# Splitting the residual addition of the last layer between ScalarE and GpSimd

## The chip, the cores and the metric

The kernel runs on one core of a Trainium2 chip. The metric is the device time of one execution in microseconds (us). Before the change it is 1846.93 us, the median of three runs (1844.24, 1846.93 and 1849.25).

## What is computed

Four layers follow one another on x, two batches of 2048 tokens of 512 values: cross attention, a routed block, a second cross attention, and a ternary feed-forward. Each is added to x behind a gate. The change is in the last one:

```python
def act_quant(x):
    scale = 127.0 / jnp.clip(jnp.max(jnp.abs(x), axis=-1, keepdims=True), 1e-05)
    return jnp.clip(jnp.round(x * scale), -128, 127) / scale
...
h = bit_linear(x, w1)                     # int8-like tokens, ternary weights, 512 -> 2048
h = depthwise_conv1d(h.transpose(0, 2, 1), conv_w, conv_b)   # three taps along the tokens
h = jax.nn.silu(h.transpose(0, 2, 1))
return bit_linear(h, w2)                  # 2048 -> 512
...
x = x + jnp.tanh(g_ffn[1]) * _L1_ffn_ref(_layernorm(x, axis=-1), ...)
```

The output product of a token has to be multiplied by that token's unit (its largest magnitude over 127, times the gate and the mean of the weights), and then added to the residual x.

## The kernel before

`ternary_layer` takes the 4096 tokens as eight tiles of 512, and a tile's 2048 hidden channels as eight pairs of 128, one pair to a **slot**. Slot p of tile n is written (n, p) here. All engines run the same double loop over n and p, each with its own instructions, and meet at semaphores. Nothing reorders them: each engine does its queue as it is written.

In a slot the work for different tiles overlaps:

- VectorE: `biggest` (line 2805) takes the maximum of the pair four slots back, from the PSUM tensor YT. `scale` (2787) moves this slot's hidden pair from PSUM to `hs`. `right_taps` (2796, two instructions, "the taps" below) adds the third tap to the pair of two slots back, reading `hs` and Y in SBUF. In slots 4 to 7, `quantise` (2823) turns one quarter of the previous tile into int8. In slots 6, 0, 2 and 4 (`ADD`), `add_out` (2831) multiplies one quarter of an output, read from its PSUM bank OP, by its unit and adds the residual R. At the end of slot 3 three small instructions (2811 to 2817) make the units.
- GpSimd: the centre tap of the even half (2697, `E_centre`), the edges (2683), and then the addition of both centre taps to Y (2705), 128 x 1024, which waits for ScalarE's taps.
- ScalarE: three taps (2724, 2731, 2734), the copy of turned tokens in slots 0 and 1 (2711), SiLU of the pair two slots back (2745), and in slots 5, 6, 7 and 0 the cast of a quarter from int8 to bf16 (`to_bf16`, 2717).
- TensorE, whose queue is about one slot ahead: `turn_y` (2629) transposes a finished pair into YT, for VectorE's `biggest`. `project_in` (2610) makes a hidden pair. In its slots 7, 1, 3 and 5, `project_out` (2620) makes a quarter of an output with 16 matmuls, in the single bank OP. It waits for the bf16 quarter and for `o_ok`, the addition that frees the bank.

The quarters of a tile's output are called c0 to c3. Those of tile n come in slots (n+1, 6), (n+2, 0), (n+2, 2) and (n+2, 4). SyncE stores a tile when its four additions are counted in `o_ok`, then loads R anew for the tile after the next. Behind the eighth tile the loops run on for two more rounds, the tail, where the last tile (n = 7) is quantised, multiplied and added.

These are the lines on which the order rests:

```python
QUANT, CAST, OUT, ADD = (4, 5, 6, 7), (5, 6, 7, 0), (7, 1, 3, 5), (6, 0, 2, 4)
...
need(pe, o_ok, SUB * n + c)                       # project_out
...
dve.wait_ge(o_mm, SUB * n + c + 1)                # add_out
dve.scalar_tensor_tensor(out=R[n % 2][:, c, :], in0=OP[:, :], scalar=f2[n % 2][:, c:c + 1],
                         in1=R[n % 2][:, c, :], op0=ALU.mult, op1=ALU.add).then_inc(o_ok, 1)
```

Of the kernel before, what the change touches and what calls it, by code (L numbers as in the profile page):

```python
# [7 lines left out]
ALU = mybir.AluOpType  # L8
ACT = mybir.ActivationFunctionType
# [2458 lines left out]
def ternary_layer(nc, io, cst, mean, last):  # L2468

    tg = cst["gates"][:, 3:4]  # L2470
    with stage_semaphores(nc, "E_") as sem, ExitStack() as ctx:
        sb = lambda n, s, d=F32: ctx.enter_context(nc.sbuf_tensor("E_" + n, s, d))
        MP, NBUF, LAG, FOLD = MC // 2, 4, 2, 4
        w1q, w2q = sb("w1q", [P, KD, DH2], BF16), sb("w2q", [P, MC, D], BF16)
        cw, cb = sb("cw", [P, MC, 3]), sb("cb", [P, MC])
# [3 lines left out]
        R = [sb(f"res{i}", [P, SUB, D]) for i in range(2)]  # L2479
        HQ, XH = sb("hq", [2 * STEPS, D], BF16), sb("xh", [P, KD, 2 * STEPS], BF16)  # L2480
        rsq, rsh, hh = sb("rs_q", [2 * STEPS, 1]), sb("rs_halo", [P, 2 * STEPS]), sb("hh", [P, MC, 2 * STEPS])
        hs = [sb(f"hs{i}", [P, 2, TILE + 2]) for i in range(NBUF)]
        U = [sb(f"centre{i}", [P, 2, TILE]) for i in range(2)]
        Y = [sb("y0", [P, MC, TILE])]
# [2 lines left out]
        a2, un, ru = sb("a2", [P, SUB]), sb("unit", [P, SUB]), sb("ru", [P, SUB])  # L2487
        mg = sb("mean_gate", [P, 1])
        f2 = [sb(f"f2_{i}", [P, SUB]) for i in range(2)]

        pb = lambda n, s, d=F32: ctx.enter_context(nc.psum_tensor("E_" + n, s, d))
        HP, YT = pb("HP", [P, 2, 2, TILE]), pb("YT", [P, SUB, 2, P])
        SBK, OP = pb("SB", [P, TILE]), pb("OP", [P, TILE])
# [10 lines left out]
        xq_in, rs_in, r_in, stored = ([sem(f"{n}{i}") for i in range(2)] for n in ("xq_in", "rs_in", "r_in", "stored"))  # L2504
        hq_in, h_tr, xh_ok, hb_mm, hh_ok = sem("hq_in"), sem("h_turned"), sem("xh_ready"), sem("halo_made"), sem("halo_kept")
        x_tr, x_te = sem("x_transposed"), sem("xT_ready")
        h_mm, h_s, h_halo = sem("h_made"), sem("h_scaled"), sem("h_edges")
        tl, ce, co, t0, t2, sil = (sem(n) for n in ("tap_left", "centre_even", "centre_odd", "taps_added", "tap_right", "silu"))
        y_tr, amk, a2_ok, un_ok, ru_ok, f_ok = (sem(n) for n in (
            "y_turned", "amax_pair", "token_max", "unit_ok", "ru_ok", "f_ok"))  # L2510
        sp_mm, q8, qb, o_mm, o_ok = sem("ru_spread"), sem("y_int8"), sem("y_bf16"), sem("out_made"), sem("out_added")

        QUANT, CAST, OUT, ADD = (4, 5, 6, 7), (5, 6, 7, 0), (7, 1, 3, 5), (6, 0, 2, 4)
        r_dr, out_dr = tile_view(io["x3_d"]), tile_view(io["out"])
# [64 lines left out]
        def _(pe):  # L2579
# [34 lines left out]
            def project_out(n, c):  # L2614

                pe.wait_ge(w2_in, 16)
                pe.wait_ge(qb, SUB * n + c + 1)
                need(pe, o_ok, SUB * n + c)
                for k in range(MC):
                    mm = pe.matmul(OP[:, :], yb[:, k, c * P:(c + 1) * P], w2q[:, k, :], start=k == 0, stop=k == MC - 1)  # L2620
                mm.then_inc(o_mm, 1)
# [55 lines left out]
        @block.gpsimd  # L2677
        def _(pool):
            def halo(n, p):

                i, t = MP * n + p, n % 2 * LAPS + n // 2
                need(pool, t2, 2 * (i - NBUF + 1))
                pool.tensor_tensor(hs[i % NBUF][:, :, 0:TILE + 2:TILE + 1], hh[:, 2 * p:2 * p + 2, t:2 * STEPS:STEPS],
                                   cst["ones"][:, 0:4].rearrange("p (a t) -> p a t", a=2), ALU.mult).then_inc(h_halo, 1)

            for c in range(SUB):
                last.scale(pool, c)
            pool.wait_ge(cw_ok, 1)
            pool.wait_ge(conv_in, 32)
            pool.wait_ge(hh_ok, 1)  # L2690
            halo(0, 0)
            for n in range(STEPS):
                for p in range(MP):
                    i = MP * n + p
                    pool.wait_ge(h_s, i + 1)
                    need(pool, t0, i - 1)
                    pool.tensor_scalar(U[i % 2][:, 0, :], hs[i % NBUF][:, 0, 1:TILE + 1], cw[:, 2 * p, 1:2],  # L2697
                                       cb[:, 2 * p:2 * p + 1], ALU.mult, ALU.add).then_inc(ce, 1)
                    if i + 1 < MP * STEPS:
                        halo((i + 1) // MP, (i + 1) % MP)  # L2700
                    pool.wait_ge(tl, 2 * (i + 1))
                    pool.wait_ge(co, i + 1)
                    pool.wait_ge(ce, i + 1)
                    y = Y[n % 2][:, 2 * p:2 * p + 2, :]
                    pool.tensor_tensor(y, y, U[i % 2][:, :, :], ALU.add).then_inc(t0, 1)  # L2705

        @block.scalar
        def _(act):
# [4 lines left out]
            def to_bf16(n, c):  # L2713
                act.wait_ge(q8, SUB * n + c + 1)
                need(act, o_mm, SUB * (n - 1) + c + 1)
                toks = slice(c * P, (c + 1) * P)
                act.activation(yb[:, :, toks], y8[:, :, toks], ACT.Copy).then_inc(qb, 1)  # L2717

            def products(n, p):
# [9 lines left out]
                if i == MP:  # L2729
# [4 lines left out]
                act.activation(Y[n % 2][:, m, :], hs[i % NBUF][:, 1, 0:TILE], ACT.Identity,  # L2734
                               bias=cb[:, m:m + 1], scale=cw[:, m, 0:1]).then_inc(tl, 1)

            def unit_out(n):
                act.wait_ge(un_ok, n + 1)
                need(act, o_ok, SUB * (n - 1))
                act.activation(f2[n % 2][:, :], un[:, :], ACT.Copy, scale=mg[:, :]).then_inc(f_ok, 1)  # L2740

            def silu(i):
# [19 lines left out]
            for n in range(STEPS + 2):  # L2762
                for p in range(MP):
                    i = MP * n + p
                    if n < STEPS:
                        products(n, p)
                    if n + 1 < STEPS and p < 2:
                        keep_xT(n + 1, p)
                    if 0 <= i - LAG < MP * STEPS:
                        silu(i - LAG)  # L2770
                    if p in CAST:
                        if p == CAST[0] and 1 <= n <= STEPS:
                            unit_out(n - 1)
                        s = n - 1 if p else n - 2
                        if 0 <= s < STEPS:
                            to_bf16(s, CAST.index(p))

        @block.vector
        def _(dve):
# [46 lines left out]

            def add_out(n, c):
                dve.wait_ge(o_mm, SUB * n + c + 1)
                dve.wait_ge(r_in[n % 2], 16 * (n // 2 + 1))
                dve.wait_ge(f_ok, n + 1)  # L2830
                dve.scalar_tensor_tensor(out=R[n % 2][:, c, :], in0=OP[:, :], scalar=f2[n % 2][:, c:c + 1],  # L2831
                                         in1=R[n % 2][:, c, :], op0=ALU.mult, op1=ALU.add).then_inc(o_ok, 1)
# [22 lines left out]
            for n in range(STEPS + 2):  # L2855
                for p in range(MP):
                    i = MP * n + p
                    if 0 <= i - FOLD < MP * STEPS:
                        biggest(i - FOLD)
                    if n < STEPS and i > 0:  # L2860
                        scale(n, p)
                    if 0 <= i - LAG < MP * STEPS:
                        right_taps(i - LAG)
                    if 1 <= n <= STEPS:
                        if p == FOLD - 1:
                            units(n - 1)
                        if p in QUANT:
                            quantise(n - 1, QUANT.index(p))
                    if p in ADD:
                        done = n - 1 if p == ADD[0] else n - 2  # L2870
                        if 0 <= done < STEPS:
                            add_out(done, ADD.index(p))


# [38 lines left out]
```

## Time and profile before

| | |
|---|---|
| median of three runs | 1846.93 us |
| the profiled execution's own time | 1849.65 us |
| its span | 1848.0 us |
| busy over the span: TensorE, VectorE, ScalarE, GpSimd | 85%, 69%, 48%, 31% |
| the last layer's tiles | from about 1465 us to the end |
| taps at line 2796 | 128, mean 874 ns |
| additions at line 2831 | 32, mean 745 ns, 23.8 us in all |
| idle time of VectorE just before them | 22.4 us, of which 15.3 us behind 1776 us |

The page gives each engine's busy time over the whole span, and the last layer is only its last fifth. So the shares of the whole say little here, and a round of eight slots in the middle of the layer is read one instruction at a time. In the timeline a row gives the start, how long it took, the engine, the line, the operation, what it writes from what it reads, and, in brackets, how long its engine stood idle before it and what ended that.

### The profile page before, as it was taken

Reading aid. Unit: us, or ns where it says so; the run is one execution under the profiler, and the core shown is the slowest. Engines: PE = TensorE matmul, PEld = TensorE weight load, DVE = VectorE, ACT = ScalarE, POOL = GpSimd, SP = SyncE. Lnnn points to the kernel's source line nnn. Section 1 sums busy time; section 2 is a strip of 40 time slices with the busy share of each in tenths; the row PEclk is TensorE's granted clock in tenths of the full one; section 3 lists DMA queues with packets and bytes.
Section 4 is the critical chain, followed back from the end, with each engine's and each line's share of the span. In section 5 each row is a group of like instructions: output and inputs, shape, how many; then the busy total and the mean of one; then the engine's idle time right before and its main releaser. Section 6 shows DMA issues by size and latency. Waiting matters only on the chain. (4 is left out here: it accounts for less than half of the span.)

```text
span 1848.0 us, 25690 instructions
## 1 busy us (share of the span) xinstructions
PE 1572.4 (85%) x9526; PEld 956.2 (52%) x9559; DVE 1272.5 (69%) x2051; ACT 890.3 (48%) x1438; POOL 580.8 (31%) x558
## 2 busy tenths in 40 slices
PE   4788889888778889747999999999998868888886
PEld 3444444443346657533666665666664534444443
DVE  3367779788542546434577766777666599999995
ACT  3355555455444436325333343333432377777763
POOL 3114332233310002113121120211201297777770
PEclk9899999999878889868999999999999899999999
DMA  4112112212623424340001211012010330222111
GB/s 157 45 47 92 65 50 71 90 69 92 243 85 102 173 95 142 119 166 22 24 24 58 68 36 59 23 58 72 9 58 29 121 120 29 70 76 77 52 46 46
DMA packets 73155, 142.34 MB, mean 77 GB/s; under 512 B 8289, under 2 KB 17653, under 8 KB 72778
## 3 DMA queue, kind: packets, MB, share of 16 engines
q1 hardware_dynamic: 72074, 137.55, 21.6%
q0 software_dynamic: 960, 3.15, 0.5%
q8 instruction: 80, 1.31, 0.3%
q14 instruction: 41, 0.34, 0.1%
HBM read 97.67 MB, written 43.01 MB: 76 GB/s over the span
## 5 line engine op out<-in xcount | busy, mean ns | idle before, releaser
L2705 POOL TENSOR_TENSOR E_y<-E_y,E_centre 128x1024 f32<-128x1024 f32 x64 | 151.2, 2362 | 9.8 <-ACT E_y L2734 7.6
L1322 ACT ACTIVATE D_oT<-D_OB 128x512 fp32r<-128x512 f32 x64 | 38.3, 598 | 226.6 <-DVE D_OB L1663 226.6
L2620 PE MATMUL E_OP<-E_w2q,E_yb 128*128 128x512 bf16 x509 | 124.8, 401 | 25.0 <-issue 18.9
L2697 POOL TENSOR_SCALAR E_centre<-E_hs,E_cw,E_cb 128x512 f32<-128x512 f32 x64 | 108.6, 1696 | 57.5 <-DVE E_hs L2787 57.2
L2610 PE MATMUL E_HP<-E_xT,E_w1q 128*128 128x512 bf16 x482 | 120.1, 388 | 2.5 <-ACT E_xT L2711 0.4
L1628 DVE TENSOR_TENSOR D_q_low<-D_PJ,D_q_high 128x512 fp32r<-128x512 f32 x62 | 42.9, 692 | 114.8 <-ACT D_q_high L1298 114.8
L1400 PE MATMUL D_PJ<-D_xT_high,D_wq_high 128*128 128x512 f32 x248 | 105.5, 425 | 9.2 <-DVE D_wq_low L1635 7.2
L2796 DVE SCALAR_TENSOR_TENSOR E_y<-E_hs,E_cw,E_y 128x512 f32<-128x512 f32 x128 | 106.9, 874 | 0.0
L2620 PEld LDWEIGHTS E_OP<-E_w2q,E_yb 128*128 128x128 bf16 x512 | 51.4, 102 | 91.9 <-issue 42.7
L1400 PE MATMUL D_PJ<-D_xT_high,D_wq_low 128*128 128x512 f32 x248 | 98.8, 399 | 0.0
L1400 PE MATMUL D_PJ<-D_xT_low,D_wq_high 128*128 128x512 f32 x248 | 98.6, 398 | 0.0
L487 PE MATMUL A_TX<-A_wo,A_oT 128*128 128x512 f32 x176 | 90.9, 642 | 7.1 <-PEq L962 7.1
L2629 PE MATMUL E_YT<-ident,E_y 128*128 128x128 f32 x512 | 68.4, 277 | 25.1 <-DVE E_am L2805 21.2
L731 ACT ACTIVATE A_probs<-A_SC 128x512 f32<-128x512 f32 x128 | 65.9, 601 | 46.9 <-PE A_SC L830 46.9
L2724 ACT ACTIVATE E_centre<-E_hs,E_cw 128x512 f32<-128x512 f32 x64 | 46.1, 720 | 84.0 <-DVE E_hs L2787 82.0
L1408 PE MATMUL D_ZB<-D_wo_high,D_oT 128*128 128x512 f32 x240 | 84.0, 411 | 2.2 <-DVE D_rz L1677 2.2
L402 POOL TENSOR_TENSOR A_rstd<-A_var,minus_half 128x1 f32<-128x1 f32 x32 | 29.8, 931 | 172.0 <-DVE A_var L541 172.0
L1408 PE MATMUL D_PJ<-D_wo_high,D_oT 128*128 128x512 f32 x240 | 80.7, 397 | 0.0
L2629 PEld LDWEIGHTS E_YT<-ident,E_y 128*128 128x128 f32 x512 | 58.5, 142 | 41.2 <-issue 20.8
L769 PE MATMUL A_PJ<-A_xT_high,A_wq_high 128*128 128x512 f32 x120 | 58.1, 484 | 25.3 <-POOL A_xT_low L648 18.6
L2787 DVE TENSOR_TENSOR E_hs<-E_HP,E_rs 128x1024 f32<-128x1024 f32 x64 | 77.5, 1211 | 2.9 <-PE E_HP L2610 2.9
L1439 PE MATMUL D_OB<-D_probs,D_V 128*32 128x512 f32 x512 | 71.7, 633 | 9.0 <-DVE D_oT L1669 9.0
(402 smaller groups left out, 4152.5 us busy)
## 6 DMA issues: line engine op xcount, KB each, us to landing
A_x<-in_x SPq DMA_DIRECT2D x8, 1024.0 KB, 5.4
A_res<-in_x SPq DMA_DIRECT2D x8, 1024.0 KB, 5.4
xn_d<-A_xn SPq DMA_DIRECT2D x8, 1024.0 KB, 4.7
x_d<-A_res SPq DMA_DIRECT2D x8, 1024.0 KB, 5.5
W_raw<-in_w1T SPq DMA_DIRECT2D x16, 512.0 KB, 3.6
W_raw<-in_w2T SPq DMA_DIRECT2D x16, 512.0 KB, 3.7
D_x<-x_d SPq DMA_DIRECT2D x8, 1024.0 KB, 5.5
D_res<-x_d SPq DMA_DIRECT2D x8, 1024.0 KB, 6.2
```

Of the source, the lines that this page charges most:

```text
L487: mm = pe.matmul(out_bank(n, c), oT[n % 2][:, k, c * P:(c + 1) * P], wo[:, k, :], start=k == 0, stop=k == QT - 1)
L731: act.activation(pr[:, g, :], SC[:, g, :], ACT.Exp, scale=scale).then_inc(s_ex, 1)
L1400: mm = pe.matmul(bank[:, :], w[:, k, m * P:(m + 1) * P], x[:, k, :], start=k == 0 and x is xh and w is wqh, stop=k == KD - 1 and x is xl)
L1408: mm = pe.matmul(bank, o[i][:, k, c * P:(c + 1) * P], w[half][:, k, :], start=k == 0 and o is oh and w is woh, stop=k == OT - 1 and o is ol)
L1439: mm = pe.matmul(OB[g * PV:(g + 1) * PV, :], V[:, par, v:v + PV], pr[:, g, :], start=True, stop=True)
L2610: mm = pe.matmul(HP[:, i % 2, e, :], w1q[:, k, m * P:(m + 1) * P], XT[n % 2][:, k, :], start=k == 0, stop=k == KD - 1)
L2620: mm = pe.matmul(OP[:, :], yb[:, k, c * P:(c + 1) * P], w2q[:, k, :], start=k == 0, stop=k == MC - 1)
L2629: mm = pe.transpose(YT[:, c, e, :], Y[i // MP % 2][:, 2 * (i % MP) + e, c * P:(c + 1) * P], ident[:, :])
L2697: pool.tensor_scalar(U[i % 2][:, 0, :], hs[i % NBUF][:, 0, 1:TILE + 1], cw[:, 2 * p, 1:2], cb[:, 2 * p:2 * p + 1], ALU.mult, ALU.add).then ...
L2705: pool.tensor_tensor(y, y, U[i % 2][:, :, :], ALU.add).then_inc(t0, 1)
L2787: dve.tensor_tensor(hs[i % NBUF][:, :, 1:TILE + 1], HP[:, i % 2, :, :], RS[n % 2][:, :].rearrange("p (a t) -> p a t", a=1).to_broadcast([P ...
L2796: dve.scalar_tensor_tensor(out=Y[n % 2][:, m, :], in0=hs[i % NBUF][:, e, 2:TILE + 2], scalar=cw[:, m, 2:3], in1=Y[n % 2][:, m, :], op0=ALU ...
```

## The change

For the first seven tiles the addition leaves VectorE. ScalarE's `scale_out` multiplies the bank OP by the unit into one of two new SBUF buffers, `scaled`. GpSimd's `add_scaled` adds that buffer to R. TensorE may refill OP when ScalarE has read it (`o_sc`), and SyncE still waits for `o_ok`, which GpSimd now counts. The last tile keeps VectorE's `add_out`. Both new steps stand at the end of their slot, in the slots of `ADD`.

```diff
+        scaled = [sb(f"out_scaled{i}", [P, D]) for i in range(2)]
...
 def project_out(n, c):
-                need(pe, o_ok, SUB * n + c)
+                if n == STEPS - 1 and c:
+                    pe.wait_ge(o_ok, SUB * n + c)
+                else:
+                    need(pe, o_sc, SUB * n + c)
...
 GpSimd
+            def add_scaled(n, c):
+                r = R[n % 2][:, c, :]
+                pool.wait_ge(o_sc, SUB * n + c + 1)
+                pool.wait_ge(r_in[n % 2], 16 * (n // 2 + 1))
+                pool.tensor_tensor(r, r, scaled[c % 2][:, :], ALU.add).then_inc(o_ok, 1)
...
                         pool.tensor_tensor(y, y, U[i % 2][:, :, :], ALU.add).then_inc(t0, 1)
+                    if p in ADD:
+                        done = n - 1 if p == ADD[0] else n - 2
+                        if 0 <= done < STEPS - 1:
+                            add_scaled(done, ADD.index(p))
...
 ScalarE
+            def scale_out(n, c):
+                act.wait_ge(o_mm, SUB * n + c + 1)
+                act.wait_ge(f_ok, n + 1)
+                need(act, o_ok, SUB * n + c - 1)
+                act.activation(scaled[c % 2][:, :], OP[:, :], ACT.Copy, scale=f2[n % 2][:, c:c + 1]).then_inc(o_sc, 1)
...
                             to_bf16(s, CAST.index(p))
+                    if p in ADD:
+                        done = n - 1 if p == ADD[0] else n - 2
+                        if 0 <= done < STEPS - 1:
+                            scale_out(done, ADD.index(p))
...
 VectorE
 def add_out(n, c):
+                dve.wait_ge(o_ok, SUB * n + c)
...
-                        if 0 <= done < STEPS:
+                        if done == STEPS - 1:
                             add_out(done, ADD.index(p))
```

GpSimd's queue over the slots 0, 1 and 2 of a tile, before (centre tap, edges, addition to Y):

```order
L2697 TENSOR_SCALAR E_centre<-E_hs,E_cw,E_cb 128x512
L2683 TENSOR_TENSOR E_hs<-E_hh,ones 128x2x2
L2705 TENSOR_TENSOR E_y<-E_y,E_centre 128x1024
L2697 TENSOR_SCALAR E_centre<-E_hs,E_cw,E_cb 128x512
L2683 TENSOR_TENSOR E_hs<-E_hh,ones 128x2x2
L2705 TENSOR_TENSOR E_y<-E_y,E_centre 128x1024
```

The same place in the changed kernel, from the addition to Y of slot 0:

```order
L2717 TENSOR_TENSOR E_y<-E_y,E_centre 128x1024
L2701 TENSOR_TENSOR E_res<-E_res,E_out_scaled 128x512
L2709 TENSOR_SCALAR E_centre<-E_hs,E_cw,E_cb 128x512
L2688 TENSOR_TENSOR E_hs<-E_hh,ones 128x2x2
L2717 TENSOR_TENSOR E_y<-E_y,E_centre 128x1024
L2709 TENSOR_SCALAR E_centre<-E_hs,E_cw,E_cb 128x512
L2688 TENSOR_TENSOR E_hs<-E_hh,ones 128x2x2
L2717 TENSOR_TENSOR E_y<-E_y,E_centre 128x1024
L2701 TENSOR_TENSOR E_res<-E_res,E_out_scaled 128x512
```

The new addition stands behind the slot's addition to Y and ahead of the next slot's centre tap, in every second slot here (slots 0, 2, 4 and 6).

ScalarE's queue in slot 0 of a tile and at the start of slot 1, in the changed kernel (2740 to 2750 the three taps, 2727 the turned tokens, 2767 SiLU, 2733 the cast):

```order
L2740 ACTIVATE E_centre<-E_hs,E_cw 128x512
L2747 ACTIVATE E_y<-E_hs,E_cw 128x512
L2750 ACTIVATE E_y<-E_hs,E_cb,E_cw 128x512
L2727 ACTIVATE E_xT<-E_SB 128x1024
L2767 ACTIVATE E_y<-E_y 128x1024
L2733 ACTIVATE E_yb<-E_y 128x16x128
L2757 ACTIVATE E_out_scaled<-E_OP,E_f_0 128x512
L2740 ACTIVATE E_centre<-E_hs,E_cw 128x512
```

The scaling stands behind the cast of quarter c3, and the next slot's taps behind the scaling. Before, the taps followed the cast at once.

## Rows read from the trace of the kernel before

**Rows 1.** Busy time in one round; columns: stretch, length, PE, PEld, DVE, ACT, POOL, PEclk, DMA, GB/s

```profile
1602.57:1647.14 44.57, 38.34 (x210) 21.02 (x212) 42.52 (x44) 32.90 (x40) 33.95 (x25) 0.96 0.18 66
```

**Rows 2.** Timeline of VectorE, (n, 0) to (n, 5), one round

```profile
1633.56 0.75 DVE L2831 SCALAR_TENSOR_TENSOR E_res<-E_OP,E_f,E_res 128x512 f32<-128x512 f32 x1 [0.61 <-PE E_OP L2620]
1634.43 1.23 DVE L2805 TENSOR_REDUCE E_am<-E_YT 128x4 f32<-128x1024 f32 x1
...
1640.30 2.64 DVE L2796 SCALAR_TENSOR_TENSOR E_y<-E_hs,E_cw,E_y 128x512 f32<-128x512 f32 x2
...
1643.54 1.23 DVE L2805 TENSOR_REDUCE E_am<-E_YT 128x4 f32<-128x1024 f32 x1
...
1645.81 1.41 DVE L2796 SCALAR_TENSOR_TENSOR E_y<-E_hs,E_cw,E_y 128x512 f32<-128x512 f32 x2
...
1650.11 1.52 DVE L2796 SCALAR_TENSOR_TENSOR E_y<-E_hs,E_cw,E_y 128x512 f32<-128x512 f32 x2
1651.55 2.27 DVE L2823 TENSOR_TENSOR E_y<-E_y,E_SB 128x2048 int8<-128x2048 f32 x1
1653.75 0.74 DVE L2831 SCALAR_TENSOR_TENSOR E_res<-E_OP,E_f,E_res 128x512 f32<-128x512 f32 x1
1654.41 1.21 DVE L2805 TENSOR_REDUCE E_am<-E_YT 128x4 f32<-128x1024 f32 x1
```

**Rows 3.** Timeline of TensorE in the same round

```profile
1617.27 5.29 PE L2620 MATMUL E_OP<-E_w2q,E_yb 128*128 128x512 bf16 x16 [3.15 <-issue]
...
1633.35 1.04 PE L2629 MATMUL E_YT<-ident,E_y 128*128 128x128 f32 x8
...
1642.46 1.04 PE L2629 MATMUL E_YT<-ident,E_y 128*128 128x128 f32 x8
```

**Rows 4.** Timeline of GpSimd, slots 1 to 4 of the same round

```profile
1636.89 1.70 POOL L2697 TENSOR_SCALAR E_centre<-E_hs,E_cw,E_cb 128x512 f32<-128x512 f32 x1 [0.75 <-DVE E_hs L2787]
...
1639.36 2.37 POOL L2705 TENSOR_TENSOR E_y<-E_y,E_centre 128x1024 f32<-128x1024 f32 x1 [0.60 <-ACT E_y L2734]
...
1643.59 2.36 POOL L2705 TENSOR_TENSOR E_y<-E_y,E_centre 128x1024 f32<-128x1024 f32 x1
...
1648.04 2.37 POOL L2705 TENSOR_TENSOR E_y<-E_y,E_centre 128x1024 f32<-128x1024 f32 x1 [0.18 <-ACT E_y L2734]
```

**Rows 5.** Timeline of GpSimd, the second centre tap of the first tile

```profile
1474.57 0.76 POOL L2697 TENSOR_SCALAR E_centre<-E_hs,E_cw,E_cb 128x512 f32<-128x512 f32 x1
```

**Rows 6.** Timeline of ScalarE, end of slot 0 and slot 1

```profile
1635.45 1.90 ACT L2717 ACTIVATE E_yb<-E_y 128x2048 bf16<-128x2048 int8 x1
1637.25 0.71 ACT L2724 ACTIVATE E_centre<-E_hs,E_cw 128x512 f32<-128x512 f32 x1
...
1638.47 0.81 ACT L2734 ACTIVATE E_y<-E_hs,E_cb,E_cw 128x512 f32<-128x512 f32 x1
```

**Rows 7.** Line 1322, ScalarE reading a PSUM bank; durations min/median/max in ns

```profile
L1322 ACT ACTIVATE D_oT<-D_OB x64: 597/597/601, 844.9 to 1445.5; 128x512 fp32r<-128x512 f32 x64
```

**Rows 8.** Line 1230, an addition on GpSimd; the same columns

```profile
L1230 POOL TENSOR_TENSOR D_res<-D_res,D_bo x32: 1260/1292/1440, 846.7 to 1412.3; 128x512 f32<-128x512 f32 x32
```

**Rows 9.** Timeline of the tail, (8, 0) to (9, 0)

```profile
1810.09 1.89 ACT L2717 ACTIVATE E_yb<-E_y 128x2048 bf16<-128x2048 int8 x1
...
1812.01 5.22 PE L2620 MATMUL E_OP<-E_w2q,E_yb 128*128 128x512 bf16 x16
...
1820.77 3.40 PE L2620 MATMUL E_OP<-E_w2q,E_yb 128*128 128x512 bf16 x15
...
1823.07 1.91 ACT L2717 ACTIVATE E_yb<-E_y 128x2048 bf16<-128x2048 int8 x1 [2.94 <-DVE E_y L2823]
...
1825.11 3.61 PE L2620 MATMUL E_OP<-E_w2q,E_yb 128*128 128x512 bf16 x16 [0.94 <-ACT E_yb L2717]
...
1830.16 3.61 PE L2620 MATMUL E_OP<-E_w2q,E_yb 128*128 128x512 bf16 x16 [1.44 <-DVE E_res L2831]
```

**Rows 10.** TensorE alone in one stretch; columns: stretch, length, PE busy, PEclk, DMA, GB/s

```profile
1617.00:1623.00 6.00, 5.73 (x22) 0.72 0.56 209
```

More of the change, by code:

```diff
@@ L2510, in ternary_layer @@
             "y_turned", "amax_pair", "token_max", "unit_ok", "ru_ok", "f_ok"))
-        sp_mm, q8, qb, o_mm, o_ok = sem("ru_spread"), sem("y_int8"), sem("y_bf16"), sem("out_made"), sem("out_added")
+        sp_mm, q8, qb, o_mm, o_sc, o_ok = (sem(n) for n in (
+            "ru_spread", "y_int8", "y_bf16", "out_made", "out_scaled", "out_added"))
         QUANT, CAST, OUT, ADD = (4, 5, 6, 7), (5, 6, 7, 0), (7, 1, 3, 5), (6, 0, 2, 4)
@@ L2691, in _ @@
             halo(0, 0)
-            for n in range(STEPS):
+            def add_scaled(n, c):
[3 more added lines that the diff above has]
+                pool.tensor_tensor(r, r, scaled[c % 2][:, :], ALU.add).then_inc(o_ok, 1)
+            for n in range(STEPS + 1):
                 for p in range(MP):
                     i = MP * n + p
[L2695 to L2705, printed above, removed]
+                    if n < STEPS:
+                        pool.wait_ge(h_s, i + 1)
+                        need(pool, t0, i - 1)
+                        pool.tensor_scalar(U[i % 2][:, 0, :], hs[i % NBUF][:, 0, 1:TILE + 1], cw[:, 2 * p, 1:2],
+                                           cb[:, 2 * p:2 * p + 1], ALU.mult, ALU.add).then_inc(ce, 1)
+                        if i + 1 < MP * STEPS:
+                            halo((i + 1) // MP, (i + 1) % MP)
+                        pool.wait_ge(tl, 2 * (i + 1))
+                        pool.wait_ge(co, i + 1)
+                        pool.wait_ge(ce, i + 1)
+                        y = Y[n % 2][:, 2 * p:2 * p + 2, :]
+                        pool.tensor_tensor(y, y, U[i % 2][:, :, :], ALU.add).then_inc(t0, 1)
+                    if p in ADD:
+                        done = n - 1 if p == ADD[0] else n - 2
+                        if 0 <= done < STEPS - 1:
+                            add_scaled(done, ADD.index(p))
         @block.scalar
@@ L2735, in products @@
                                bias=cb[:, m:m + 1], scale=cw[:, m, 0:1]).then_inc(tl, 1)
+            def scale_out(n, c):
[3 more added lines that the diff above has]
+                act.activation(scaled[c % 2][:, :], OP[:, :], ACT.Copy, scale=f2[n % 2][:, c:c + 1]).then_inc(o_sc, 1)
             def unit_out(n):
                 act.wait_ge(un_ok, n + 1)
-                need(act, o_ok, SUB * (n - 1))
+                need(act, o_sc, SUB * (n - 1))
                 act.activation(f2[n % 2][:, :], un[:, :], ACT.Copy, scale=mg[:, :]).then_inc(f_ok, 1)
```

## The prediction

> **What bounds the kernel now.** I read the page first (the last layer is the last fifth of the span), then the busy time of one round, then the waits of VectorE in it, then the timelines of the five engines over that round, because a share of busy time does not say which of two nearly full engines a slot waits for.
>
> In a round of eight slots VectorE is busy for 42.5 of 44.6 us, TensorE for 38.3, GpSimd for 34.0 and ScalarE for 32.9 [rows 1]. By these sums an addition taken from VectorE, four of them in a round, should shorten it. The timelines say otherwise, in three ways.
>
> First, **two of the four additions stand in a shadow of TensorE**. The addition of c1 waited 0.61 us for its product and began at 1633.56, and the next `biggest` began at 1634.43, just when TensorE had turned a pair for it: that transpose ran from 1633.35 to 1634.39, behind the product [rows 2, 3]. Without the addition `biggest` begins at the same moment. c0 behaves in the same way one slot after its product, and its product is late because the cast before it is late (3.15 us idle ahead of it) and because it took 5.29 us where others take 3.61 [rows 3, 9]. The granted clock was 0.72 in that stretch [rows 10], against 0.96 over the round [rows 1].
>
> Second, c2 is in a shadow too. `biggest` of slot 3 began at 1643.54, and the transpose for it ended at 1643.50 [rows 2, 3].
>
> Only c3 is in the open: 1653.75 to 1654.41, 0.66 us, with its transpose long done [rows 2].
>
> Third, **GpSimd and the taps exclude each other**. The two taps of a slot take 1.41 us together, but 2.64 us where they began at 1640.30 under GpSimd's addition to Y, which ran from 1639.36 to 1641.73. They ended 1.21 us behind its end, as if they had begun just about there [rows 2, 4]. The addition itself is never longer than its 2.36 us. The other way round, the centre tap takes 1.70 us when it begins with VectorE's taps (1636.89, the usual case), and 0.76 us when it does not [rows 4, 5]. `biggest`, `scale`, `quantise` and `add_out`, which read at most one operand from SBUF (the other is in PSUM), keep their durations under GpSimd's work. In slots 1 to 4 GpSimd has hardly any slack: its addition of slot 2 ends at 1645.95, when the taps of slot 3 (1645.81) begin, and that of slot 3 at 1650.41, when the taps of slot 4 (1650.11) do, which already costs them 0.11 us [rows 2, 4].
>
> **The change, part by part.** The price of each new step: the scaling on ScalarE, between 0.60 us (a read of a PSUM bank without a scale by token, [rows 7]) and 0.71 us (a tap with a scale by partition, [rows 6]). I take 0.65. The addition on GpSimd reads two operands from SBUF: between 1.18 us (half of 2.36, [rows 4]) and 1.44 us, with a median of 1.29 [rows 8]. I take 1.27. Taken away: 28 additions of 0.66 us on VectorE, 18.5 us of engine time, of which by the above only the seven of c3 lie open, and c1 to c3 of the seventh tile lie in the tail.
>
> Now one round, in the times of the trace, from an undisturbed slot 7 on.
>
> - Slot 0, ScalarE. The scaling of c1 stands behind the cast of c3, which ends at 1637.35 [rows 6], though its product was done at about 1633.4. So it runs from 1637.3 to 1637.95. Slot 1's taps follow at 1637.95, 0.7 us late, and end at 1639.98 instead of 1639.28.
> - GpSimd stands idle at the end of slot 0 for the scaling. Its addition of c1 runs from 1638.0 to 1639.3, where slot 1's centre tap began at 1636.89. The centre tap, now outside the taps, takes 0.76 and the edges 0.2, so the addition to Y begins at about 1640.25 instead of 1639.36 and ends at 1642.6.
> - VectorE's taps of slot 2 come at 1640.30, 0.05 us behind it, and are held until 1642.6. They end 1.21 us later, at 1643.8, and `biggest` begins at 1643.75 (instructions of VectorE overlap by 0.08 us, [rows 2]): 0.2 us late.
> - GpSimd, slot 2: centre tap under the held taps 1.70, edges 0.2, addition to Y from 1644.5 to 1646.85. VectorE's taps of slot 3, due at 1646.0, are held until then, and end at 1648.06 instead of 1647.22: 0.85 us late.
> - GpSimd adds c2 from 1648.05 to 1649.3, centre tap and edges to 1650.3, addition to Y to 1652.65. VectorE's taps of slot 4, due 4.30 us behind those of slot 3 [rows 2], now at 1650.97, are held until 1652.65. `quantise` begins at 1653.8 instead of 1651.55: **2.25 us late**. If GpSimd's addition of c2 goes ahead of the held taps of slot 3 instead of behind, the taps of slot 3 lose 1.25 us more and those of slot 4 as much less, with the same sum within 0.2 us.
> - Then c3's addition is missing, 0.66 us. Slot 5 begins **1.6 us later than before**. GpSimd's addition of c3 ends about when slot 5's taps begin, and GpSimd has caught up by slot 6. From slot 5 on the cast of c0, its product and slot 7 follow VectorE's `scale` at fixed distances, so nothing takes the loss back.
>
> What GpSimd's delay and the held taps cost is thus 2.25 us, what is saved 0.66, net 1.55 to 1.6 in a round. The slots 0 to 4 with these additions come in the rounds of tiles n = 2 to 7: 6 x 1.55 = **9.3 us**. The ends of the range: with the cheap prices (0.60 and 1.18) GpSimd is 0.14 us earlier behind c1 and another 0.09 behind c2: 1.3 net, 7.9 us. With the costly ones (0.71 and 1.44) it is 0.23 and 0.17 later, and if VectorE is first by a hair at 1640.30, GpSimd waits there for one tap or both (0.7 to 1.4 us) and passes on what VectorE did not lose, some 0.5: 2.45 net, 14.7 us.
>
> The row on the centre tap can be weighed against a rule. The Trainium skill (SBUF — State Buffer, Who interferes with whom) says that a VectorE instruction with two SBUF inputs and a GpSimd instruction that reads SBUF exclude each other, and that the second to start is blocked fully until the first ends. For the taps the trace agrees (2.64 us). By it a centre tap under both taps would take 1.2 + 0.76 = 1.99 us, where the row has 1.70. The sum here goes by the row; by the rule each round would lose 0.3 us more, 1.8 us in all, and the estimate would be about 1860 us.
>
> **The tail.** The product of c2 of the seventh tile began at 1812.01. Its bank is now free when c1 has been scaled, behind the cast that runs from 1810.09 to 1811.98 [rows 9]: 1812.6. That passes through the last units to the product at 1820.77, 0.7 us later. Then the scaling of c3 (slot 4) stands in ScalarE's queue ahead of the first cast of the last tile (slot 5), and waits for that product: it ends at 1825.1, is read to 1825.8, and the cast that ran from 1823.07 ends at 1827.7. The product that began at 1825.11 begins at about 1827.8, and the next one, at 1830.16 before, waits for its addition and begins at 1832.3 [rows 9]. That is **2.1 us**; behind it the chain is as before. SyncE's store and the load of R move with `o_ok` by two or three us, and R is used a tile later.
>
> **The sum.** 9.3 + 2.1 = 11.4 us on the profiled execution, 1849.65 to about 1861. The median of the runs is 2.7 us lower; I add to that: 1846.93 + 11.4 = **1858.3 us**. With the ends of the terms this case alone spans 1855 to 1864.
>
> **The rivals.** A measurement of this kernel tells about 0.3%, 5.5 us, from no change.
>
> 1. *The clock steps in further.* TensorE stands idle longer in each round, and the product that begins after an idle stretch took 1.68 us more at the lower clock [rows 3, 9]. If a second product in each of six rounds, one on the chain (c1 or c2), does so: 10 us more, 1868. For it: one round already has 0.96 on the mean [rows 1]. Against it: of the round's four products only c0's is behind an idle stretch of 3 us.
> 2. *GpSimd keeps in time.* If the new additions cost the taps nothing more, because the order at 1640.30 and 1646 falls well or the scaling comes earlier than I think, each round gains the 0.66 of c3: 6 x 0.66 = 4.0, less 2.1 in the tail, 1845: no difference. It decides at whether GpSimd's addition to Y in slots 2 and 3 ends less than 0.2 us behind the start of the taps. Against it: 5 us of port time per round are added to a stretch without slack.
> 3. *Faster.* As 2, and TensorE, freed from waiting for VectorE, is moved so that c0's product runs at full clock in five rounds: 1.68 x 5 = 8.4 us, 1837. Or VectorE's busy time is the bound after all and the 18.5 us show, 1828. For it: 42.5 of 44.6 us busy. Against it: the shadows above; VectorE's 2.05 us of idle in the round are waits for TensorE, and they grow when an addition in a shadow goes.
>
> **Chances.** The forecast 0.52; rival 1 0.13; rival 2, or the forecast at less than half its size, 0.22; rival 3 0.13. So faster 0.13, same 0.22, slower 0.65. The predicted time is the forecast's. The range goes from rival 2's 1845 to rival 1's 1868 and leaves out rival 3 and little more.
>
> **What would show it.** In the changed profile: VectorE has 4 additions of R left, mean duration of the taps above 874 ns with several pairs of 2 to 3 us in slots 2, 3 and 4; GpSimd idle about 1.9 us before the addition of c1, waiting for ScalarE, with that addition at 1.2 to 1.4 us; rounds of about 46.1 us between the units; `biggest` of slot 1 still beginning at the end of a transpose; c0's product still at 5.3 us. The first cast of the last tile begins right behind a scaling. I am wrong if the rounds come out below 44.6 us: then either the taps were not held, or the additions were not in a shadow.

## The result, and the profile after

The changed kernel takes 1863.2 us, the median of seven runs (1859.44 to 1868.36), and the kernel before takes 1849.25 us, the median of seven beside them. The ratio is 1.0077, with a 95% interval from 1.0056 to 1.0098: 14 us slower, where 11.4 were forecast. The profiled execution took 1866.61 us, with a span of 1864.6 us. It is one of the three of the seven with a mean granted clock of 0.923 to 0.926 (1866.61 to 1868.36 us); the other four, at 0.931 to 0.933, took 1859.44 to 1863.2, so the profile shows more of the low clock than the median execution has.

First the busy time of two rounds that follow one another, with the same columns as [rows 1], from units to units:

```profile
1610.34:1657.19 46.85, 39.87 (x208) 21.46 (x212) 42.33 (x40) 35.51 (x43) 37.83 (x29) 0.93 0.20 63
1657.19:1702.62 45.43, 38.13 (x208) 20.87 (x212) 42.26 (x41) 35.40 (x43) 37.84 (x29) 0.96 0.19 64
```

Against 44.57 us in [rows 1], the rounds are 2.3 and 0.9 us longer. VectorE has lost its additions and is as busy as it was (42.3 against 42.5): 0.2 us less, not 2.6. GpSimd has gained 3.9 us and ScalarE 2.6. From the first units to the seventh the six rounds sum to 276.3 us, where they were 262.5: 13.8 us more. Their mean is 46.05 us, and the forecast said about 46.1, but that agreement is luck: the forecast added 1.55 to the 44.57 of [rows 1], while the six rounds of before are 43.74 us on the mean, so that 2.3 us were added to each.

The timeline of VectorE and GpSimd over slots 1 to 4 answers to [rows 2, 4]. It begins in the first of these rounds and passes into the second at 1657.19:

```profile
1642.68 1.23 DVE L2831 TENSOR_REDUCE E_am<-E_YT 128x4 f32<-128x1024 f32 x1 [1.48 <-PE E_YT L2634]
...
1646.26 1.27 POOL L2701 TENSOR_TENSOR E_res<-E_res,E_out_scaled 128x512 f32<-128x512 f32 x1 [1.86 <-ACT E_out_scaled L2757]
...
1647.51 0.78 POOL L2709 TENSOR_SCALAR E_centre<-E_hs,E_cw,E_cb 128x512 f32<-128x512 f32 x1
...
1648.46 2.36 POOL L2717 TENSOR_TENSOR E_y<-E_y,E_centre 128x1024 f32<-128x1024 f32 x1
1648.54 3.49 DVE L2822 SCALAR_TENSOR_TENSOR E_y<-E_hs,E_cw,E_y 128x512 f32<-128x512 f32 x2
...
1652.68 2.36 POOL L2717 TENSOR_TENSOR E_y<-E_y,E_centre 128x1024 f32<-128x1024 f32 x1
...
1654.22 3.05 DVE L2822 SCALAR_TENSOR_TENSOR E_y<-E_hs,E_cw,E_y 128x512 f32<-128x512 f32 x2
...
1655.00 1.72 POOL L2701 TENSOR_TENSOR E_res<-E_res,E_out_scaled 128x512 f32<-128x512 f32 x1
1656.71 1.21 POOL L2709 TENSOR_SCALAR E_centre<-E_hs,E_cw,E_cb 128x512 f32<-128x512 f32 x1
...
1660.32 1.41 DVE L2822 SCALAR_TENSOR_TENSOR E_y<-E_hs,E_cw,E_y 128x512 f32<-128x512 f32 x2
```

Five things can be read in it. `biggest` of slot 1 waits 1.48 us for TensorE's transpose, where the wait for c1's product and its addition stood before (0.61 and 0.75 us, [rows 2]): that addition was in a shadow. GpSimd stands idle for 1.86 us until c1 is scaled. Its addition to Y of slot 1 begins 0.08 us ahead of the taps of slot 2, which take 3.49 us instead of 2.64. In slot 3 the taps come first at 1654.22, but are held by the addition to Y until 1655.04. Then they and the addition of c2 take turns: the addition takes 1.72 us where 1.27 is usual, the taps 3.05 where 1.41 is. And in slot 4 they are free.

The clock shows in TensorE's products. This is its timeline: c2, c3 and then c0 of the next tile, in the round ahead and in this one, with the spreading of the units in front of c3's:

```profile
1600.40 3.62 PE L2625 MATMUL E_OP<-E_w2q,E_yb 128*128 128x512 bf16 x16
...
1611.36 0.65 PE L2643 MATMUL E_SB<-ident,E_ru 128*128 128x128 f32 x4 [1.96 <-DVE E_ru L2843]
1611.84 5.30 PE L2625 MATMUL E_OP<-E_w2q,E_yb 128*128 128x512 bf16 x16
1625.52 5.30 PE L2625 MATMUL E_OP<-E_w2q,E_yb 128*128 128x512 bf16 x16 [3.15 <-issue]
...
1647.26 3.62 PE L2625 MATMUL E_OP<-E_w2q,E_yb 128*128 128x512 bf16 x16
...
1658.20 0.65 PE L2643 MATMUL E_SB<-ident,E_ru 128*128 128x128 f32 x4 [1.95 <-DVE E_ru L2843]
1658.69 3.62 PE L2625 MATMUL E_OP<-E_w2q,E_yb 128*128 128x512 bf16 x16
1671.30 4.93 PE L2625 MATMUL E_OP<-E_w2q,E_yb 128*128 128x512 bf16 x16 [3.15 <-issue]
```

The windows of TensorE alone over c3's product in the two rounds, with the columns of [rows 10] (stretch, length, PE busy, PEclk, DMA share, GB/s):

```profile
1612.00:1618.00 6.00, 6.00 (x25) 0.72 0.01 4
1657.19:1663.19 6.00, 4.98 (x28) 1.00 0.00 0
```

c3's product at 1611.84 took 5.30 us at a granted clock of 0.72 (a mean over full and half speed), the one at 1658.69 took 3.62 us at 1.00. In the six rounds of before only c0's product was ever at the low clock. Now c0's is in five rounds, c3's in two and c1's in one. In these rounds the products' time above 3.62 us sums to 13.7 us (8 products, 9.0 us of it c0's, one of which took 6.56 us), against 6.2 us (4 products, all c0's) before.

### The profile page after: what moved, and what is told of

It is laid out like the page before. It is cut to its first block and busy times, and to the rows that moved or that the text cites. A ratio compares the mean times of both kernels' runs of the same rounds, so it can differ in the third digit from the quotient of the medians.

```text
span 1864.6 us, 25750 instructions
## 1 busy us (share of the span) xinstructions
PE 1582.7 (85%) x9526; PEld 960.6 (52%) x9559; DVE 1267.6 (68%) x2023; ACT 908.0 (49%) x1466; POOL 610.1 (33%) x586
## 3 DMA queue, kind: packets, MB, share of 16 engines
q0 software_dynamic: 960, 3.15, 0.5%
## 5 line engine op out<-in xcount | busy, mean ns | idle before, releaser
L2625 PE MATMUL E_OP<-E_w2q,E_yb 128*128 128x512 bf16 x509 | 131.8, 418 | 27.6 <-issue 18.9
L2822 DVE SCALAR_TENSOR_TENSOR E_y<-E_hs,E_cw,E_y 128x512 f32<-128x512 f32 x128 | 121.5, 988 | 0.0
L2709 POOL TENSOR_SCALAR E_centre<-E_hs,E_cw,E_cb 128x512 f32<-128x512 f32 x64 | 99.3, 1551 | 30.9 <-DVE E_hs L2813 30.0
L2831 DVE TENSOR_REDUCE E_am<-E_YT 128x4 f32<-128x1024 f32 x64 | 77.8, 1216 | 29.7 <-PE E_YT L2634 29.7
L2740 ACT ACTIVATE E_centre<-E_hs,E_cw 128x512 f32<-128x512 f32 x64 | 46.1, 720 | 72.2 <-DVE E_hs L2813 57.8
L1208 POOL TENSOR_TENSOR D_rstd<-D_var,minus_half 128x4 f32<-128x4 f32 x8 | 8.2, 1028 | 214.1 <-DVE D_var L1555 214.1
```

The costliest lines, as they stand in the source:

```text
L2822: dve.scalar_tensor_tensor(out=Y[n % 2][:, m, :], in0=hs[i % NBUF][:, e, 2:TILE + 2], scalar=cw[:, m, 2:3], in1=Y[n % 2][:, m, :], op0=ALU ...
L2831: dve.tensor_reduce(am[:, :, i % MP], YT[:, :, :, :].rearrange("p c e x -> p c (e x)"), AX.X, ALU.max, apply_absolute_value=True).then_inc ...
```

## The experiments

All kernels below but the change with the added matmuls use one rewritten place: the bank OP is released by whoever has read it, and the additions on GpSimd are counted apart.

```diff
+        MOVED = [(n, c) for n in range(STEPS) for c in range(SUB) if ...]   # which quarters go to ScalarE and GpSimd
 project_out
+                need(pe, o_sc, SUB * n + c)          # o_sc: the bank has been read, by either engine
```

**GpSimd's addition made narrow** (only 4 of 512 columns are added, the rest of R is left out).

```diff
-                r = R[n % 2][:, c, :]
-                pool.tensor_tensor(r, r, scaled[c % 2][:, :], ALU.add)
+                r = R[n % 2][:, c, 0:4]
+                pool.tensor_tensor(r, r, scaled[c % 2][:, 0:4], ALU.add)
```

> The changed kernel, but GpSimd's new addition takes 4 columns of 512 (the other 508 columns of the residual addition are left out of the first seven tiles). Its waits and its place in the queue stay. Theory A (the addition holds the port that the taps want, and makes GpSimd late): between the units of two tiles the rounds fall from 45.4 and 46.9 us to 44.6 +- 0.4, the taps of slot 3 from 3.05 to at most 2.1 us, those of slot 2 from 3.5 to 3.3. Theory B (what delays is ScalarE's scaling and the wait for it, not the addition): rounds stay at 45.4 or above. Theory C (the clock, from TensorE's idle time, is most of the loss): the products of c3 keep taking 5.3 us in half of the rounds, and the time stays within 3 us of the change's. Time by A: the kernel before + 3 us, ratio 1.002; by B 1.006; by C 1.007.

Measured: ratio 1.0013 (1.0003 to 1.0023). The busy time of one round, and VectorE's timeline in slots 2 and 3 of it, in this kernel:

```profile
1605.32:1649.83 44.51, 38.56 (x213) 21.06 (x212) 40.94 (x40) 35.18 (x44) 33.63 (x29) 0.96 0.19 66
```

```profile
1642.45 3.23 DVE L2822 SCALAR_TENSOR_TENSOR E_y<-E_hs,E_cw,E_y 128x512 f32<-128x512 f32 x2
...
1647.97 1.94 DVE L2822 SCALAR_TENSOR_TENSOR E_y<-E_hs,E_cw,E_y 128x512 f32<-128x512 f32 x2
```

Theory A holds. The taps of slots 2 and 3 are still longer than before (3.23 and 1.94 us): that is the lateness that ScalarE's scaling and the wait for it leave, and it uses up just what c3 saves. c3's product is at full clock in every round here, with 0.83 us of idle time of TensorE ahead of the spreading. Theory C does not hold: it had the 5.3 us products of c3 stay.

**The addition on GpSimd alone.**

```diff
 kernel before, GpSimd, in the slots of ADD
+                            q = scaled[ADD.index(p) % 2][:, :]
+                            pool.tensor_tensor(q, q, q, ALU.add)
```

> The kernel before in everything that computes (VectorE keeps its 32 additions), plus 28 additions of 128 x 512 on GpSimd that nobody waits for, scratch onto scratch, in the places of the change's additions. Theory A: the port and GpSimd's time alone do the damage: rounds 1.0 to 1.5 us longer than 44.5, taps of slots 2 and 3 at 2.6 to 3.5 us, ratio 1.004 to 1.007. Theory B (scaling and wait): rounds as before, ratio 1.000 to 1.001.

Measured: ratio 1.0070 (1.0051 to 1.0089). Behind the first, which is 43.2 us long, the rounds take 45.4, 45.2, 44.0, 46.7 and 45.0 us. VectorE's timeline, taps of slots 1, 2 and 3:

```profile
1639.69 1.66 DVE L2827 SCALAR_TENSOR_TENSOR E_y<-E_hs,E_cw,E_y 128x512 f32<-128x512 f32 x2
...
1643.54 2.40 DVE L2827 SCALAR_TENSOR_TENSOR E_y<-E_hs,E_cw,E_y 128x512 f32<-128x512 f32 x2
...
1648.80 2.19 DVE L2827 SCALAR_TENSOR_TENSOR E_y<-E_hs,E_cw,E_y 128x512 f32<-128x512 f32 x2
```

Nobody reads this result and nobody waits for it, and the kernel's loss cannot be told from the change's. So GpSimd's time at these places costs something by itself. The expected place of it was missed in part: the taps of slots 2 and 3 take 2.40 and 2.19 us (2.6 to 3.5 expected), those of slot 2 even less than the 2.64 of before, and those of slot 1 now 1.66 instead of 1.41. At like clock the loss in a round is 0.8 us (43.97 against 43.14, both with c0's product at full clock). One product of c0 took 6.54 us in this profile, and 2.3 us more arose between the seventh and the eighth units, so the 1.0070 is not the held taps alone.

**One quarter at a time.** `MOVED` holds one quarter of the tiles 0 to 5.

> Only c1 of the tiles 0 to 5 is moved (scaled at the end of slot 0, added by GpSimd at the end of slot 0), the other quarters stay on VectorE. Theory A, from the rows: ScalarE's taps of slot 1 are 0.7 us late, GpSimd waits for the scaling, its addition to Y of slot 1 is 0.9 us late and that of slot 2 too, so the taps of slot 2 take 3.5 us and those of slot 3 about 2.1: rounds 0.75 us longer than 44.5. Nothing is saved, since c1 stands in TensorE's shadow. Ratio 1.0025. Rival: the addition was not in a shadow and its 0.66 us come back, rounds at 44.5.

> Only c2 of the tiles 0 to 5 is moved (added by GpSimd at the end of slot 2). Theory A: the taps of slot 2 stay at 2.6 us and nothing is saved there; GpSimd's addition follows its addition to Y just as the taps of slot 3 begin and goes ahead of one of the two, so that they take 2.7 us instead of 1.4: rounds 1.2 us longer than 44.5, ratio 1.004. If it waits behind both taps instead, the taps of slot 4 are held and the sum is the same within 0.3 us. Rival: the damage comes only where c1 has made GpSimd late before, and rounds stay at 44.5.

> Only the quarter c3 of the tiles 0 to 5 is scaled on ScalarE and added on GpSimd, c0 to c2 stay on VectorE, as all of the last two tiles. Theory A (c3 is the only addition in the open, and it comes where GpSimd has 2 us of slack): 0.66 us less in each of six rounds, rounds about 43.8 us, 4 us less than the kernel before, ratio 0.998. Theory D (an addition on GpSimd costs wherever it stands): rounds at 44.5 or longer, ratio 1.000 or above. If the clock moves a product, 1.7 us for each.

> c0 and c3 of the tiles 0 to 5 are moved, c1 and c2 and all of the last two tiles stay on VectorE. Both additions come where GpSimd stood idle (2.1 us behind slot 4, 3.5 us behind slot 6). Theory A: c3 saves 0.6 us in a round; c0 is in the shadow of a product at the low clock, and saves 0.6 us only in rounds in which that product runs at full clock. Rounds 43.9, time as with c3 alone or up to 1 us less, ratio 0.997. Rival: every addition on GpSimd costs port time, rounds at 44.5, ratio 1.000.

| moved | ratio to the kernel before (95%) | round | taps of slots 2, 3 | expected round |
|---|---|---|---|---|
| c1 | 1.0037 (1.0024 to 1.0050) | 45.4 to 45.5, c0 at low clock (46.6 and 45.9 where its product took 6.5 and 6.6) | 3.48, 1.40 | 45.2 |
| c2 | 1.0036 (1.0012 to 1.0061) | 44.2, c0 at full clock in five rounds | 2.64, 2.42 | 45.7 |
| c3 | 0.9973 (0.9960 to 0.9986) | 43.9, c0 at low clock | 2.65, 1.41 | 43.8 |
| c0 and c3 | 0.9991 (0.9982 to 1.0000) | 43.9, c0 at low clock (at full clock 44.4, with c1's product slow, and 41.8) | 2.64, 1.41 | 43.9 |

The busy time of one round in the kernel with c2 alone:

```profile
1651.25:1695.45 44.20, 37.11 (x212) 20.57 (x212) 42.80 (x44) 33.59 (x40) 35.33 (x26) 1.00 0.19 66
```

The same with c3 alone:

```profile
1648.31:1692.24 43.93, 38.55 (x214) 21.08 (x212) 41.89 (x43) 33.49 (x41) 35.06 (x26) 0.96 0.19 67
```

The table has to be read at like clock. In the kernel before, one round had c0's product at full clock:

```profile
1559.43:1602.57 43.14, 36.91 (x210) 20.55 (x212) 42.34 (x45) 32.91 (x40) 34.12 (x25) 1.00 0.21 68
```

Beside it c2 costs 1.1 us in a round. Beside the rounds of 44.5 us with c0 at the low clock, c1 costs 0.9 to 1.0, and c3 saves 0.6. The three together are a loss of 1.4 to 1.5 us, where the forecast walk had 1.55 to 1.6. For c1 I had expected the taps of slot 3 held too; they were not, and nearly all of the loss sits in slot 2.

With c0's product at the low clock c0 saves nothing, as expected. Where its product was at full clock 0.6 us had been expected from it, and it did not come. There GpSimd's addition of c0 (from 1711.78, 1.28 us) holds the taps of slot 7, which take 1.86 us instead of 1.41:

```profile
1712.42 1.86 DVE L2822 SCALAR_TENSOR_TENSOR E_y<-E_hs,E_cw,E_y 128x512 f32<-128x512 f32 x2
```

The last of the six rounds, with every product at full clock, takes 41.75 us, where the kernel with c3 alone and all products at full clock (the last one below) takes 41.55: c0 costs 0.2 us there. The times (0.9991 against 0.9973, intervals that overlap) are too close to settle more.

**The additions moved to slots in which GpSimd is idle.**

```diff
-                    if p in ADD: ... add_scaled(done, ADD.index(p))
+                    for c, slot, back in ((1, 4, 2), (2, 5, 2), (3, 6, 2), (0, 6, 1)):
+                        if p == slot and (n - back, c) in MOVED:
+                            add_scaled(n - back, c)
 SyncE
+                    load_rows(n + 1)        # ahead of the store of its round, four buffers of scaled
```

> All 28 additions on GpSimd, but c1, c2 and c3 of a tile in slots 4, 5 and 6 instead of 0, 2 and 4 (four buffers; SyncE loads the next rows ahead of its store), where GpSimd stands idle for 1.4 to 3.5 us between slots. ScalarE's scalings stay where the change has them. Theory A (the place of GpSimd's work decides): rounds 44.7 +- 0.4, the taps of slot 3 at most 2.2 us, ratio 1.001 to 1.003. Theory E (the added port time of 5 us in a round has to be paid wherever it stands): rounds stay at 45.4 or more, ratio 1.006. Theory B (ScalarE's scalings): as E in time, but with the taps of slots 2 and 3 at 3.5 and 3 us.

Measured: ratio 1.0004 (0.9992 to 1.0016). The busy time of one round, and the timeline of the moved additions on GpSimd in it (its last row is two additions), with VectorE's taps of slot 7:

```profile
1608.81:1653.41 44.60, 38.56 (x214) 21.05 (x212) 40.03 (x40) 35.37 (x44) 38.70 (x29) 0.96 0.19 66
```

```profile
1616.34 1.28 POOL L2705 TENSOR_TENSOR E_res<-E_res,E_out_scaled 128x512 f32<-128x512 f32 x1
...
1622.21 1.26 POOL L2705 TENSOR_TENSOR E_res<-E_res,E_out_scaled 128x512 f32<-128x512 f32 x1
...
1628.03 2.49 POOL L2705 TENSOR_TENSOR E_res<-E_res,E_out_scaled 128x512 f32<-128x512 f32 x2
...
1629.65 2.09 DVE L2825 SCALAR_TENSOR_TENSOR E_y<-E_hs,E_cw,E_y 128x512 f32<-128x512 f32 x2
```

The taps of slots 2 and 3 in the fifth of the six rounds:

```profile
1735.09 3.21 DVE L2825 SCALAR_TENSOR_TENSOR E_y<-E_hs,E_cw,E_y 128x512 f32<-128x512 f32 x2
...
1740.60 1.94 DVE L2825 SCALAR_TENSOR_TENSOR E_y<-E_hs,E_cw,E_y 128x512 f32<-128x512 f32 x2
```

The additions are the same (GpSimd is busy for 38.7 us in a round, VectorE for 40.0), and the loss is gone. The place decides, not the sum. There is no gain either, and where c3's 0.6 us go depends on the product that was slow. In the second to fourth round it was c1's (5.30 us, c0's at full clock): there the two additions in slot 6 hold the taps of slot 7 (2.09 us instead of 1.40). In the first and in the last two rounds the scaling delays ScalarE, and the taps of slots 2 and 3 take 3.1 to 3.2 and 1.9 to 2.1 us, as with the narrow addition. The clock does not hide a loss here: from the second round on one product in each round was at the low clock, five in all (8.4 us above 3.62) against four (6.2 us) before, and the six rounds sum to 264.7 us against 262.5.

**The tail as before.** `MOVED` holds all quarters of the tiles 0 to 5.

> The change without its last moved tile: tiles 0 to 5 are moved, tile 6 stays on VectorE like tile 7. Rounds as in the change, 45.4 and, with c3's product at the low clock, 46.9 us, except that the last one (1749 to 1795 there) loses nothing at c1 and c2. Theory A: the first product of the last tile begins 4.3 us behind the product of c3 of tile 6, as in the kernel before, instead of 6.2 us; time 2 us below the change's from the tail and 1 us from the last round, ratio to the kernel before 1.006. Rival: the tail was no loss (it measured only 0.4 us longer than before), and the time is 1 us below the change's at most.

Measured: ratio 1.0068 (1.0047 to 1.0089), not apart from the change's. The first product of the last tile began 6.2 us behind c3's as in the change, but for another reason: c3's product took 5.30 us here. What the tail costs by itself is not settled by this run.

The run settles something else. All additions in its six rounds are those of the tiles 0 to 5 (the expectation, which has the last of these rounds lose less, is mistaken in that), so over these rounds the engines do what they do in the changed kernel, in another execution. They sum to 271.6 us, 9.2 more than before and 4.7 less than in the change's profile. c3's product stayed at full clock in every one, behind the same idle time of up to 1.95 us; c1's was at the low clock in two rounds and c0's in three (8.1 us above 3.62 in all). So which products run slowly, and how many, can differ between executions of the same work.

**TensorE kept busy.** Matmuls whose result is overwritten go into the free bank OP ahead of c0's product; in the changed kernel six also ahead of c3's.

```diff
+            def idle_matmuls(n, c, count):
+                need(pe, o_sc, SUB * n + c)
+                for _ in range(count):
+                    pe.matmul(OP[:, :], w2q[:, 0, 0:P], w2q[:, 1, :], start=True, stop=True)
 project_out
+                if c == 0 and n < STEPS - 1:
+                    idle_matmuls(n, c, 10)
                 pe.wait_ge(qb, SUB * n + c + 1)
```

> The kernel before with ten matmuls of 512 columns, whose result is overwritten, into the free bank OP ahead of c0's product, where TensorE stands idle for 3.15 us. Clock theory (the product that follows the idle stretch runs at the low clock because TensorE was idle): c0's product takes 3.62 us in every round, rounds 43.1 instead of 44.5, about 6 us less in all, ratio 0.997. Rival: the clock falls for another reason, the low stretch comes elsewhere in the round, and rounds stay at 44.5, ratio 1.000.

> The change with the same ten matmuls ahead of c0's product, and six ahead of the spreading of the units in front of c3's product, where TensorE stood idle for 1.95 us. Clock theory: half of the change's loss is TensorE's clock (products at the low clock cost 13.7 us in its six rounds against 6.2 us before), so all products take 3.62 us, rounds 44.0 to 44.4, 10 to 13 us less than the change, ratio to the kernel before 1.000 to 1.002, and 1.003 to 1.004 to the kernel before with its own added matmuls: what is left is the held taps. Rival (the clock follows something else): products at 5.3 us remain in half of the rounds, ratio 1.006.

> Only c3 of the tiles 0 to 5 moved, with the ten matmuls ahead of c0's product. Clock theory and the shadow together: rounds 42.5 us, 12 us less in all than the kernel before, ratio 0.994. Rival: the clock falls elsewhere in the round, rounds 43.9, ratio 0.997 as without the matmuls.

| kernel | ratio to the kernel before (95%) | rounds 3 to 5 | six rounds |
|---|---|---|---|
| before, with the matmuls | 0.9962 (0.9949 to 0.9976) | 43.13 | 257.2 us |
| change, with the matmuls | 1.0019 (1.0008 to 1.0031) | 44.55 | 267.3 us |
| c3 alone, with the matmuls | 0.9940 (0.9917 to 0.9963) | 42.49 | 253.9 us |

TensorE's timeline in the kernel before with the matmuls, these ten and c0's product behind them:

```profile
1614.51 2.32 PE L2624 MATMUL E_OP<-E_w2q 128*128 128x512 bf16 x10
1617.78 3.63 PE L2634 MATMUL E_OP<-E_w2q,E_yb 128*128 128x512 bf16 x16 [0.95 <-ACT E_yb L2742]
```

It takes 3.63 us, where [rows 3] has 5.29, though 0.95 us of idle time are left. So the clock of this product follows what TensorE did ahead of it. Between the two kernels with the matmuls, 10.0 us are left of the 13.8 in six rounds, 1.42 us in each of the three later ones, where every product is at full clock: that is GpSimd's place and the held taps. The clock falls as the main cause and stands as a part: 3.8 us by this comparison. That is the lower end, for one product of the change was still slow (c1's in the second round, 5.30 us, where all were expected at 3.62). Counting the products' excess (13.7 less 6.2) gives 7.5; a slow product may lie partly beside other work, so I take this for the upper end.

The expectation had put half of the loss on the clock, and that was too much. Rounds of 44.0 to 44.4 us were expected in the change with the matmuls, and they took 44.55. Beside the kernel before with its matmuls a ratio of 1.003 to 1.004 was expected, and 1854.10 against 1843.93 us is 1.0055.

The last kernel is the fastest of all: 1839.19 us beside 1851.56 for the kernel before.

## Why the prediction was right

**The shadows.** Right. c3 alone saves 0.55 to 0.64 us in a round (0.66 forecast), c0 with it saves no more, and c1 or c2 alone only cost.

**The walk up to the taps of slot 3.** Right to 0.1 us. Set the trace's slot 0 (taps at 1639.80) on the forecast's (1631.54), 8.26 us apart. The addition of c1 was forecast for 1638.0 + 8.26 = 1646.26, and began at 1646.26. Slot 1's addition to Y: 1648.51 forecast, 1648.46 measured. The pair of taps in slot 2: 3.5 us, 3.49. Scaling 0.67 us (0.65 taken), the addition 1.27 (1.27).

**Slots 3 and 4.** Here the forecast had both taps ahead of the addition of c2, and named the addition ahead of both as the other order. In fact they take turns: tap, addition, tap. So slot 3 lost more than forecast, and the taps of slot 4 were free where 1.7 us were forecast. `quantise` began at 1661.66, 1.85 us late instead of 2.25, and slot 5 at 1663.86, 1.2 instead of 1.6. The prediction had said that the order changes the sum by 0.2 us at most; it was 0.4 in this round. And the loss did not simply stand from slot 5 on: with c0's product at full clock GpSimd's addition of c0 holds the taps of slot 7 (1.88 us instead of 1.40 in the change with the matmuls), which adds 0.2 us a round that the forecast did not have.

**The clock.** The term that the sum put at nothing. It stood as rival 1 with 13%, for a second product on the chain, c1's or c2's, in each round. It came in three rounds of six, twice with c3's product and once with c1's. Ahead of the spreading, which stands in front of c3's product, the late units let TensorE stand idle for 1.95 us, where it had stood idle for 0.14 (between 1647.85 and 1647.99 in the trace of before); with the narrow addition it was 0.83. The wait does not decide alone. It was 1.43 us at the second round's start and 1.95 us from then on, and c3's product was at the low clock in every other round; in the kernel with the tail as before, which does the same work in these rounds, it never was. That the late units alone bring c3's slow product is thus not shown. What is shown is that keeping TensorE busy takes nearly all slow products away: none is left in the six rounds of two of the kernels with the matmuls, and one in the third. Of the 7.5 us that the slow products took more than before, 4.6 were those of c1 and c3 and 2.8 those of c0 itself, slow in one round more and once for 6.56 us.

**The sum.** 9.3 us were forecast for the six rounds, 13.8 measured. At like clock the held taps, net of what c3 saves, cost less than forecast: 1.2 us in a round with c0's product at the low clock (45.43 against 44.48, and 0.25 for c0's product, 4.93 against 5.18), 1.42 at full clock, where 1.55 was forecast. As an estimate from these rounds, that is 7.2 to 8.5 us in six; the kernel with the tail as before gives 7.3 (9.2, less 1.9 for slow products). The other 5.3 to 6.6 us of the profile are clock. So the mechanism and the order of size were right, and part of the nearness of 11.4 to the measured 14 is luck: the walk was 1 to 2 us too large, the tail came to 0.4 instead of 2.1, and the clock, at nothing in the sum, more than made up for both. The result, 1863.2 us, lies half way between the forecast, 1858.3, and the end of the range, 1868, that rival 1 had set; 2.3 of the 4.9 us above the forecast are the kernel before, 1849.25 us in seven runs against the 1846.93 of three.

Two slips in the prediction's sums changed nothing in it. The low end of the forecast's own case, 1855, leaves out the tail; with it it is 1857 (1846.93 + 7.9 + 2.1). And 1.2 + 0.76 is 1.96, not 1.99.

**The tail.** Forecast at 2.1 us; behind the seventh units it was 0.4 us longer. The cast did wait for the scaling, in the changed kernel's timeline of ScalarE and TensorE:

```profile
1839.46 0.69 ACT L2757 ACTIVATE E_out_scaled<-E_OP,E_f 128x512 f32<-128x512 f32 x1 [6.24 <-PE E_OP L2625]
...
1842.23 3.61 PE L2625 MATMUL E_OP<-E_w2q,E_yb 128*128 128x512 bf16 x16 [2.81 <-ACT E_yb L2733]
```

The first product of the last tile came 6.2 us behind the start of c3's (1836.02), against 4.3 in [rows 9]. But the product of c2 ahead of it took 3.61 us, where it had taken 5.22 [rows 9]: 1.6 us were given back by the clock. So the tail's mechanism was right, and its effect was hidden. The remaining 2.4 us of the span arose ahead of the first units (1519.44 against 1517.04), ahead of the first moved addition. In the profiles of the other kernels the first units come anywhere from 1514.09 to 1521.20 us, so no cause in the change is needed for them.

**The rule on the port** (the Trainium skill, SBUF — State Buffer, Who interferes with whom: the second to start is blocked fully) fits the taps: 3.49 us is 2.28 until the addition's end and 1.21 for both. (The port is the access to SBUF that the taps and GpSimd's instructions exclude each other from.) For a centre tap that meets both taps the row stays at 1.71 us and not 1.99, so the rule's extra 0.3 us a round did not come. The addition of c2 had 1.72 us, about its 1.27 and one tap (0.7) less some overlap: the port changes hands between two taps of a pair. The rule does not say so; here it shows in slot 3 of all rounds but the first, with taps of 3.05 or 3.06 us.

## What to carry to other kernels

Before work is moved off the busiest engine, look for each piece at what the next instruction waits for: of four equal pieces here only one was in the open, and moving that one alone gave 0.27%. The receiving engine's busy share says little; what matters is whether it has slack at that place, and whether its instruction and the neighbour's exclude each other there. Where TensorE idles ahead of a long product, its clock is part of the price of every delay, and cheap matmuls into a free bank can be worth more (0.38%) than the rearrangement. And because slow products fall differently in each execution, compare rounds only at like clock: read the products first, then the round.

## What was not expected of the hardware

VectorE and GpSimd, both waiting for the port, take turns by instruction: tap, addition, tap, with 1.72 us for an addition of 1.27. A centre tap on GpSimd takes 0.78 us alone, 1.21 us when it meets one tap and 1.71 us when it meets two. And the low clock does not need the longest idle stretch: c3's product fell to it behind 1.95 us of idle time, at 5.30 us, but only in every second round, and in another execution of the same work not at all, while in the kernel with c2 alone c0's product kept the full clock, at 3.61 us, five times in a row behind its usual wait of 3.15 us.
